# Two buffers for the pieces of an expert table, and routing and first fetches put elsewhere, in an attention and expert kernel on one core

## The reference

```python
x = layernorm(x + attention(x, wq, wk, wv, wo))     # x is (8, 512, 512), f32
                                                    # 16 query heads, 4 key heads, head size 128, causal
x = layernorm(x + ffn(x))

def ffn(x):                                         # xt: 4096 tokens x 512
    logits = clip(xt @ gate_w.T, -50, 50)           # 8 experts
    top_w, top_idx = top_k(logits, 2); rw = softmax(top_w)
    deltas = softmax(expert_atom_weights) @ atoms   # 8 x 4096
    weighted = deltas * sigmoid(importance)
    # each expert is a sparse 512 x 512 matrix: entry s stands at
    # row mask_idx[s] // 512, column mask_idx[s] % 512
    contrib[t] = sum over the 2 experts of rw * (sparse matrix of the expert @ xt[t])
    return xt @ W.T + contrib
```

## Time and profile before

| | before |
|---|---|
| median of 3 runs | 2000.81 us (1997.71 to 2002.41) |
| profiled execution, its own time | 1998.23 us |
| its span, first to last instruction | 1996.4 us |
| mean granted TensorE clock, as a share of full speed | 0.958 |
| busy, of the span | PE 93%, DVE 62%, POOL 46%, ACT 39% |

### The profile page before, as it was taken

The page is one execution under the profiler, slowest core; times in us unless marked ns, Lnnn a source line. Parts: engine busy times, 40 slices in busy tenths (PEclk is TensorE's granted clock), DMA queues, the critical chain, the costliest instruction groups (busy, mean ns, idle before and its releaser), DMA issues.

```text
span 1996.4 us, 34047 instructions
## 1 busy us (share of the span) xinstructions
PE 1855.9 (93%) x9525; PEld 1569.1 (79%) x9525; DVE 1228.6 (62%) x3786; ACT 778.1 (39%) x1985; POOL 925.7 (46%) x1282
## 2 busy tenths in 40 slices
PE   7899999999999999999998999999899988899990
PEld 7788888888888888888887778877788866677770
DVE  4445557776677677667756776677767764543435
ACT  1244444443434444344433333433434432233442
POOL 6366434334443444343435554554432335677763
PEclk6899999999999999999999999999999989899995
DMA  8453363334333433343355554655443285345766
GB/s 287 164 175 121 117 243 117 117 106 149 106 111 101 149 111 122 116 139 106 117 175 154 169 169 148 197 165 163 153 159 139 75 317 195 127 146 201 262 228 269
DMA packets 151974, 318.77 MB, mean 160 GB/s; under 512 B 18904, under 2 KB 62184, under 8 KB 140840
## 3 DMA queue, kind: packets, MB, share of 16 engines
q1 hardware_dynamic: 132320, 273.06, 40.0%
q0 software_dynamic: 19472, 43.49, 7.0%
HBM read 226.38 MB, written 90.12 MB: 159 GB/s over the span
## 4 chain that ended last, share of the span: by engine, by line
PE 64%; POOL 9%; DVE 7%; issue 6%; DMA 6%; ACT 2%; SPq 1%; POOLq 1%; DVEq 0%; ACTq 0%
PE psum L1245 18%; PE psum L1247 17%; PE psum L1246 17%; PE psum L1272 5%; DMA route_rows<-attn_residual 2%; POOL piece_lo L1165 2%; ACT probs L1496 2%; DMA split_expert_weights<-piece_lo 2%; PE psum L1882 2%; PE psum L1883 2%; PE psum L1884 2%; POOL piece_hi L873 1%; POOL token_rows L270 1%; DMA token_rows<-x,ids_now 1%; POOL expert_slots L470 1%
## 5 line engine op out<-in xcount | busy, mean ns | idle before, releaser
L1135 POOL TENSOR_SCALAR probs<-probs,row_inv 128x128 f32<-128x128 f32 (+3 forms) x512 | 306.5, 630 | 422.7 <-DVE row_inv L1598 420.0
L1496 ACT ACTIVATE probs<-probs,neg_max 128x512 f32<-128x512 f32 (+3 forms) x512 | 282.5, 554 | 366.5 <-DVE neg_max L1590 364.4
L1245 PE MATMUL psum<-xT_hi,w_hi 128*128 128x512 f32 x640 | 253.1, 395 | 7.1 <-PEq L622 3.7
L1247 PE MATMUL psum<-xT_hi,w_lo 128*128 128x512 f32 x640 | 250.9, 392 | 0.0
L1246 PE MATMUL psum<-xT_lo,w_hi 128*128 128x512 f32 x640 | 250.4, 391 | 0.0
L1590 DVE CUSTOM_DVE_ANT_0 probs<-psum,causal 128x512 f32<-128x512 f32 (+3 forms) x512 | 223.1, 487 | 32.7 <-PE psum L1247 12.3
L1245 PE MATMUL psum<-wo_hi,oT_hi 128*128 128x512 f32 x512 | 208.3, 407 | 27.0 <-DVE y_acc L1625 26.5
L1601 DVE TENSOR_TENSOR pT_lo<-psum,pT_hi 128x512 fp32r<-128x512 f32 (+1 forms) x384 | 206.5, 593 | 22.6 <-ACT pT_hi L1506 22.3
L1506 ACT CAST pT_hi<-psum 128x512 fp32r<-128x512 f32 (+1 forms) x384 | 172.2, 526 | 90.4 <-PE psum L1272 90.4
L1247 PE MATMUL psum<-wo_hi,oT_lo 128*128 128x512 f32 x512 | 203.9, 398 | 0.0
L1246 PE MATMUL psum<-wo_lo,oT_hi 128*128 128x512 f32 x512 | 203.7, 398 | 0.0
(11 more groups left out here) (200 smaller groups left out, 4054.6 us busy)
## 6 DMA issues: line engine op xcount, KB each, us to landing
w_hi<-split_qk_weights SPq DMA_DIRECT2D x140, 256.0 KB, 2.8
w_lo<-split_qk_weights SPq DMA_DIRECT2D x140, 256.0 KB, 3.2
wo_hi<-split_out_weights SPq DMA_DIRECT2D x28, 1024.0 KB, 4.9
wo_lo<-split_out_weights SPq DMA_DIRECT2D x28, 1024.0 KB, 7.1
expert_weights_hi_lo<-split_expert_weights SPq DMA_DIRECT2D x8, 2048.0 KB, 9.7
x_in<-in_L_attn_x_dram SPq DMA_DIRECT2D x8, 1024.0 KB
expert_weights<-fill_sb SPq DMA_DIRECT2D x4, 2048.0 KB, 8.7
attn_residual<-y_acc SPq DMA_DIRECT2D x8, 1024.0 KB
```

The source lines that it names most:

```text
L1135: last = pool.tensor_scalar(p, p, row_inv[:, buf, i:i + 1], 1.0, ALU.mult, ALU.mult)
L1245: pe.matmul(dst, hi_s, hi_m, start=start, stop=False)
L1247: return pe.matmul(dst, lo_s, hi_m, start=False, stop=stop)
L1496: last = act.activation(probs[:, buf, a:a + w], probs[:, buf, a:a + w], ACT.Exp, bias=neg_max[:, buf, i:i + 1], scale=-1.0, accum_out=row_ ...
```

## The change

1. `piece_hi` and `piece_lo` get two buffers (`piece_raw` moves to other memory to make room), and each store counts on its own semaphore, so that POOL waits for the store of two pieces ago. SP issues the stores of both pieces after its three weight slots, where the first stood between them.
2. On POOL, `normalize(n + 4, 0)` stands ahead of `split_v` and `low_v`, in every iteration that has both.
3. On DVE in the last batch, the three parts of the tile table stand at the ends of the iterations g = 0, 1, 2; before, in the middle of g = 1, 2, 3.
4. In the very last iteration POOL issues the four first token fetches near its top rather than at its end; ACT and DVE make `pT(n + 3)` earlier, ahead of parts of the routing; and the hi and lo parts of the first token tile are made at the iteration's end rather than in the stage of the experts. The buffers of that tile lie in the memory of `causal` and of `v_hi`.
5. In the stage of the experts, one DVE copy of a 128x2 slot (destination and share together, `slot_now`, eight buffers) takes the place of POOL's copy of the destination (L268) and DVE's copy of the share. The last four token tiles are routed in six turns each instead of five: PE's ranks at step 5 instead of 4, DVE's ranks and places at 6 instead of 5, POOL's `route_place` at 7 instead of 6. PE's wait for the last `y_acc` is at the third tile instead of the second.
6. In the tail, the shift of a pair is computed after the variance of the next one.

Left out of the diff: the declarations of the buffers, semaphores and their memory, the same change of wait at two more places, and the new names in `send`, `rows_out` and the matmuls.

```diff
 JT = SEGMENTS * SEG_TILES
-AHEAD, TOKEN_BUFS = 2, 3
+AHEAD, TOKEN_BUFS, SLOT_BUFS = 2, 3, 8
 BANK_RANK, BANK_TURN, BANK_ROWS = 0, 1, 4
...
+def high_tokens(act, E, psum, j):
+
+    act.wait_ge(E.s_turn, j + 1)
+    act.copy(E.xT_hi[j % TOKEN_BUFS][:], psum[:, BANK_TURN + j % 2, :]).then_inc(E.s_hi, 1)
+
+
+def low_tokens(dve, E, psum, j):
+
+    number = dve.value_load(E.tile_number_i[0:1, j:j + 1], min_val=0, max_val=SEG_COLS - 1)
+    dve.wait_ge(E.s_hi, j + 1)
+    dve.tensor_copy(E.slot_now[:, j % SLOT_BUFS], slot_column(E, j, number).rearrange("p a n -> p (a n)")
+                    ).then_inc(E.s_slot_now, 1)
+    dve.tensor_tensor(E.xT_lo[j % TOKEN_BUFS][:], psum[:, BANK_TURN + j % 2, :], E.xT_hi[j % TOKEN_BUFS][:].bitcast(F32),
+                      ALU.subtract).then_inc(E.s_lo, 1)
+
+
 def slot_column(E, j, number):
...
-    k, buf, segment = j % GROUP, j // GROUP % 2, j // SEG_TILES
+    k, segment = j % GROUP, j // SEG_TILES
     if j >= 2 * GROUP:
...
     pool.tensor_copy(E.ids_now[:, k:k + 1], E.token_ids[:, segment, bass.ds(number, 1)]).then_inc(E.s_ids_now, 1)
-    pool.tensor_copy(E.dest_now[:, buf, k:k + 1], slot_column(E, j, number)[:, :, 0]).then_inc(E.s_ids_now, 1)
-    pool.wait_ge(E.s_ids_now, 2 * j + 2)
+    pool.wait_ge(E.s_ids_now, j + 1)
     pool.indirect_dma_start(out=E.token_rows[:, k], out_offset=None,
...
     s_piece_in = [sem(f"piece_{k}_loaded") for k in range(2)]
-    s_piece, s_piece_out = sem("piece_split"), sem("piece_kept")
+    s_piece, s_piece_out = sem("piece_split"), [sem(f"piece_{k}_kept") for k in range(2)]
...
                 dst = kept_pieces[bass.ds((b - SPLIT_BATCHES[0]) * 2 + step // PER_C, 1), step % PER_C, s]
-                sp.dma_start(dst.rearrange("a p e r -> (a p) e r"), half[:].bitcast(F32)).then_inc(s_piece_out, 16)
+                sp.dma_start(dst.rearrange("a p e r -> (a p) e r"), half[:, step % 2].bitcast(F32)
+                             ).then_inc(s_piece_out[step % 2], 16)
...
                 slot(j, it + 2, second)
-                if job == "split" and j == 0:
-                    keep_piece(b, 2 * g)
             if job == "split":
-                keep_piece(b, 2 * g + 1)
+                for half in range(2):
+                    keep_piece(b, 2 * g + half)
             if job == "last":
                 if g == 0:
-                    sp.wait_ge(s_piece_out, 32 * PIECES)
+                    for kept in s_piece_out:
+                        sp.wait_ge(kept, 16 * PIECES)
                     sp.wait_ge(s_v, NB * TT)
...
         def split_piece(b, g, step):
-            number = piece_number(b, step)
-            raw = F.piece_raw[:, step % 2].rearrange("p (r e) -> p e r", e=NE)
-            wait_apart(pool, s_piece_in[step % 2], 16 * ((b - SPLIT_BATCHES[0]) * HKV + g + 1), s_passed)
-            wait_apart(pool, s_piece_out, 32 * number, s_passed)
-            pool_round(pool, F.piece_hi[:], raw).then_inc(s_piece, 1)
+            number, k = piece_number(b, step), step % 2
+            raw = F.piece_raw[:, k].rearrange("p (r e) -> p e r", e=NE)
+            wait_apart(pool, s_piece_in[k], 16 * ((b - SPLIT_BATCHES[0]) * HKV + g + 1), s_passed)
+            wait_apart(pool, s_piece_out[k], 32 * ((b - SPLIT_BATCHES[0]) * HKV + g), s_passed)
+            pool_round(pool, F.piece_hi[:, k], raw).then_inc(s_piece, 1)
             wait_apart(pool, s_piece, 2 * number + 1, s_passed)
-            pool.tensor_tensor(F.piece_lo[:], raw, F.piece_hi[:].bitcast(F32), ALU.subtract).then_inc(s_piece, 1)
+            pool.tensor_tensor(F.piece_lo[:, k], raw, F.piece_hi[:, k].bitcast(F32), ALU.subtract).then_inc(s_piece, 1)
...
             normalize(n + 1, 1)
+            if kind == "end":
+                pool.wait_ge(E.s_ids, 1)
+                pool.wait_ge(E.s_tables, 1)
+                pool.wait_ge(R.s_x1_out, 16 * (SEG_T + 1))
+                for j in range(GROUP):
+                    fetch(pool, R, E, j)
             if kind == "first" and route:
...
                 slot(j, it + 2)
+            if kind != "end":
+                normalize(n + 4, 0)
             if kind in ("first", "group"):
...
                 low_v(g + 1, it + 2)
-            if kind != "end":
-                normalize(n + 4, 0)
             if not route and kind == "batch":
...
             if job == "last" and g == 0:
+                for kept in s_piece_out:
+                    pool.wait_ge(kept, 16 * PIECES)
                 pool.iota(table.tile_at_i[:], pattern=[[1, SEG_TILES]], base=0, channel_multiplier=0).then_inc(E.s_tile_at, 1)
-            if kind == "end":
-
-                pool.wait_ge(E.s_ids, 1)
-                pool.wait_ge(E.s_tables, 1)
-                pool.wait_ge(R.s_x1_out, 16 * (SEG_T + 1))
-                for j in range(GROUP):
-                    fetch(pool, R, E, j)
             if route:
...
                 qT(n + 5, 1, bank_of_query(1, kind))
+            if kind == "end":
+                pT(n + 3, 1)
             if route:
                 route_exp(act, R, it - TT)
-            pT(n + 3, 1)
+            if kind != "end":
+                pT(n + 3, 1)
             oT(n, 1, kind)
...
                 exps(n + 4, 0)
+            else:
+                high_tokens(act, E, psum, 0)
...
             inverse(n + 2, 0)
-            if job == "last":
-                if g == 1:
-                    table_sums_low(dve, E, table)
-                if g == 2:
-                    table_behind(dve, E, table)
             if early:
...
             inverse(n + 3, 1)
-            if kind == "end":
-                table_numbers(dve, E, table)
             if route:
...
             oT(n, 0, 0, kind)
+            if kind == "end":
+                pT(n + 2, 0)
             if route:
...
             if kind == "end":
-                pT(n + 2, 0)
                 add_rows(it - 1, 3, "spare")
             oT(n, 0, 1, kind)
+            if kind == "end":
+                pT(n + 3, 1)
             if route:
...
                 qT(n + 5, 1, bank_of_query(1, kind))
-            pT(n + 3, 1)
-            if kind != "end":
+                pT(n + 3, 1)
                 maxima(n + 4, 0)
...
                 inverse(n + 4, 0)
+            else:
+                low_tokens(dve, E, psum, 0)
             if job == "last" and g == 1:
...
                 add_rows(it, 3, kind)
+            if job == "last" and g < HKV - 1:
+                (table_sums_low, table_behind, table_numbers)[g](dve, E, table)
...
     y_pairs = y_dram[0:2 * CAP, :].rearrange("(c u p t) d -> c u p t d", c=2, p=P, t=2)
-    B, FIRST_ROUTED, ROUTE_STEPS, FIRST_PAIR = SEGMENTS - 1, 4, 5, 11 * GROUP
-    COUNTED = FIRST_ROUTED + ROUTE_STEPS * TT + 3
+    B, FIRST_ROUTED, ROUTE_STEPS, FIRST_PAIR = SEGMENTS - 1, 4, 6, 11 * GROUP
+    COUNTED = FIRST_ROUTED + ROUTE_STEPS * (TT - 1) + 7
     s_used_pool = sem("c_rows_used_by_pool")
...
             step = i - FIRST_ROUTED - ROUTE_STEPS * (tt - LAST)
-            if 0 <= step <= 6:
+            if 0 <= step <= 7:
                 yield tt, step
...
             for tt, step in routed(j):
-                if step == 6:
+                if step == 7:
                     route_place(pool, R, tt)
...
                     pe.wait_ge(E.s_d_in[e], 16)
-            if j == 1:
+            if j == 2:
...
             for tt, step in routed(j):
-                if step == 4:
+                if step == 5:
                     route_ranks(pe, R, tt, B, upper, ones, BANK_RANK)
...
     def scalar(act):
-        def high(j):
-            act.wait_ge(E.s_turn, j + 1)
-            act.copy(E.xT_hi[:, j % TOKEN_BUFS].rearrange("p c n -> p (c n)"), psum[:, BANK_TURN + j % 2, :]).then_inc(E.s_hi, 1)
-
         def rows_out(j):
...
                 act.wait_ge(E.s_y_out[k], 16 * (j // GROUP))
-            act.wait_ge(E.s_share_now, j + 1)
-            act.activation(E.y_rows[:, k], psum[:, BANK_ROWS + k, :], ACT.Copy, scale=E.share_now[:, k:k + 1]).then_inc(E.s_y_sb, 1)
+            act.wait_ge(E.s_slot_now, j + 1)
+            act.activation(E.y_rows[:, k], psum[:, BANK_ROWS + k, :], ACT.Copy, scale=E.slot_now[:, j % SLOT_BUFS, 1:2].bitcast(F32)).then_inc(E.s_y_sb, 1)
...
-        for j in range(AHEAD):
-            low(j)
+        for j in range(1, AHEAD):
+            low_tokens(dve, E, psum, j)
         for j in range(JT):
             if j + AHEAD < JT:
-                low(j + AHEAD)
+                low_tokens(dve, E, psum, j + AHEAD)
             for tt, step in routed(j):
...
                     route_shares(dve, R, tt)
+                if step == 6:
                     route_ranked(dve, R, tt, B, BANK_RANK)
...
             variance(u)
-            shift_of(u)
+            if v:
+                shift_of(u - 1)
+        shift_of(PAIRS + PAIRS_LEFT - 1)
```

(21 more changed lines are left out.)

30 lines of the change are left out of this document (11 added, 19 removed).

## The result

The changed kernel takes 2009.04 us (median of 7 runs, 2007.54 to 2011.42), the kernel before 2000.07 in the same comparison (7 runs, 1997.71 to 2003.02). The ratio is 1.0045, with a 95% interval from 1.0033 to 1.0057: slower by 9 us. The profiled execution took 2008.11, with a span of 2006.3.

The account below looks back on a forecast made before the run. TensorE, busy 1855.9 of 1996.4 us, was taken as the bound, with its waits and lower clock to change. Terms 12.8 + 21.0 - 12 - 3.5 - 5 - 3 + 1 = +11.3 on 1998.23 gave 2009, range 1972 to 2020.

Parts of the forecast that it names:

- Pieces: Split batches 5 and 6: two buffers end the late store, but the second piece holds up DVE; 54.8 instead of 42.0, +12.8 us.
- case A: Rival as summed: DVE is held up by both pieces and by `v_lo`; 2009 us, 2001 to 2020, split batch 218; chance 0.42.
- stall of 4.0 per iteration: Split batches: PE idles 4.0 us in each of four iterations behind held-up L530 and `qT_lo`, plus 1.8 for the clock.
- Order of v: Iteration ends: `v_lo` behind normalize holds up DVE's L563; 1.4 us per iteration, +21.0 outside the split batches, bounds 0 to 22.5.
- Six turns and the copy: Experts' stage: -12 us for four routed tiles (-5 to -15), and -3.5 in turns that carry pairs (0 to -5).
- 0.15 a turn: Experts' stage, turns with pairs: POOL sets the pace in part of them; 23 turns by 0.15, -3.5 us.
- Tail: Shift one pair later removes the wait for `c_rstd` in 7 of 8 pairs; -5 us, between -2 and -7.
- which stays: Tail: POOL's addition holds up other operations, two `c_shift` taking 1.29 us, and this was to remain after the change.
- Turn into the experts and tables: Last batch: earlier token fetches -3 us (-2 to -8); table pieces moved to iteration ends +1 (-2 to +2).
- B: Rival: hold-ups exist, but L530 runs before `piece_lo` and costs nothing; 2000 us, or 1986 with half the v term; chance 0.28.
- C: Rival: idle PE comes from the late store, and the second piece finds DVE's gaps; 1963 us, 1934 to 1979; chance 0.20.
- D: Rival: POOL's waiting and placing per tile keep it behind despite six turns; -5 for -12, 7 us higher; chance another 0.06.

Follow-up runs that it names:

- experiment 1: Kernel before with only the two piece buffers, their waits and the stores behind the weight slots: 2008.08 us, ratio 1.0041.
- experiment 4: Changed kernel with v split ahead of normalize again and POOL's second piece waiting for DVE's conversion and chosen experts: 1946.81 us, ratio 0.9742 against the kernel before.
- experiment 5: Changed kernel with v split ahead of normalize again and, in split batches, DVE's routing and ACT's exponential later: 1934.43 us, ratio 0.968 against the kernel before.
- experiment 9: Kernel before, one piece buffer, with only the routing moved later on DVE and ACT in the split batches: 2003.26 us, ratio 1.0029.
- experiment 3: Changed kernel with the split of v ahead of normalize(n+4,0) again: 1983.64 us, ratio 0.9919 against the kernel before.
- experiment 2: Kernel before with only normalize(n+4,0) moved ahead of the split of v: 2020.34 us, ratio 1.0105.
- experiment 6: Changed kernel with the last four token tiles routed in five turns each again: 2016.01 us, ratio 1.0088 against the kernel before.
- experiment 10: Changed kernel with v split ahead of normalize again and the four first token fetches back at the last iteration's end: 1987.44 us, ratio 0.9945 against the kernel before.
- experiment 8: Changed kernel with the tile table's three parts in the middle of the last batch's iterations again: 2021.3 us, ratio 1.012 against the kernel before.

## Why the prediction was right

2009.04 was measured where 2009 was forecast, and that agreement is luck. The forecast added 11.3 us to the profiled execution's 1998.23; measured are 9.0 between the medians, from 2000.07. And terms that were off by 1 to 4 us cancel within the sum. What the experiments bear out is the account.

- **Pieces.** +12.8 forecast, +11.9 in the two windows, a split batch at 218.2 and 217.8 where case A had 218. The stall of 4.0 per iteration measured 3.8, L530 held up for 2.74 as in case A, and experiments 1, 4, 5 and 9 show the mechanism from both sides. Within a split batch I had 4.2 us for the order of v and 4 x 5.8 = 23.2 for the stall with its lower clock; set against the changed kernel, experiments 1 and 3 give 1.8 to 4.1 for the one and 23.1 to 25.3 for the other. The sign that the busy time rises at a lower clock held: 198.98 at 0.96 against 190.83 at 1.00 in the earlier trace rows. One reading behind the step was wrong: the 0.69 of `qT_lo` in the earlier trace rows does not show that what reads PSUM is not held up, since POOL stood idle beside it. The `pT_lo` of experiment 5 show it.
- **Order of v.** 1.4 forecast for an iteration, 1.33 measured (15.9 / 12). The step named the wrong victim: not the conversion (L563) but the rank product ahead of it was held up, by 1.1 us; the 0.2 of the first rank product was forecast. I had taken the times of the earlier trace rows as fixed, while `v_lo` came at the very moment of the product. In the last batch the term is larger than its 4.2: 7 us in experiment 2, of which 1.6 may not be its doing, and 6.1 between the changed kernel and experiment 3, part of it in the turn into the experts.
- **Six turns and the copy.** -12 and -3.5 forecast; -6.2 and -3.5 by the means under experiment 6, -8.3 and -3.1 by single executions, with the second holding more than the copy. The sum of the stage is -11.4, not -15.5: the first is a term that I sized too large, and its 2.1 for each of the last three tiles came from no row. The 23-tile window hid this: its -11.6 is partly given back behind it, where experiment 6 is 3.5 us faster than the changed kernel. I had also taken the stage to end at 1955, while the last product ends at 1946.2. The window held 8.8 us of the tail, and PE's idle time in the 55 tiles is 7.0 us, not 15.8. The 0.15 a turn that I took for POOL's pace had thus less to work on than I thought, and no run separates it.
- **Tail.** -5 forecast, -8.4 measured, outside my bounds of -2 to -7. The failing step is "which stays": the hold-up of `c_shift` by POOL's addition does not stay, since in its new place it runs during the gap ahead of that addition. A pair costs 2.92 and not 3.5 us. It is the same hold-up as in the rest of the kernel, and I did not carry it through here.
- **Turn into the experts and tables.** -3 and +1 forecast; the fetches' place measures -2.2 to -3.3 (experiment 10). The tables' +1 could not be measured by itself (experiment 8).
- **The rivals.** B and C both hung on L530. It was held up in all eight iterations, so they are out. The prediction's D, that six turns would give 5 us and not 12, was at least as near as A: 6.2, or 8.3 at the most.

With the routing moved out of the pieces' way and v split first, the rest of the change is worth 64 us (1934.43).

What the trace shows of L542, L544, L546 and L577 is what the Trainium skill ("SBUF — State Buffer", section "Who interferes with whom") states: copies, casts and tensor_scalar in two-port modes, and operations of two SBUF inputs beside a GpSimd operation that reads SBUF, are blocked for the whole of a GpSimd operation that issued first. Held up here are a tensor_scalar (L542), a cast (L546) and two operations of two SBUF inputs (L544, L577), each to the end of a GpSimd operation that had begun before it (L546 at 1137.23, behind `piece_lo` at 1137.10). By the same section of the Trainium skill a DVE operation with at most one SBUF input, outside the two-port modes, does not contend with GpSimd. The `pT_lo` beside the pieces in experiment 5 agree (0.67 to 0.68 us), and the maximum L543, which has one SBUF input, was not held up either (0.17 us beside `piece_hi`).

## What to carry to other kernels

A wait that keeps two engines apart can be what protects them from each other: before it is removed, lay the freed work on the other engine's timeline and look at which small operations it will lie on, and at what stands behind these in order. When an engine's busy time rises with the same number of instructions, compare the durations of the small operations by line, and compare their ends with those of the neighbour's large operations. If the transfer can't move, the small operations can: the same early pieces cost 23 to 25 us a batch with the routing beside them, and nothing with it moved behind the second one.

## What the hardware showed that I had not expected

A 128x2 conversion that takes 0.17 us stood for 2.74 us, and the price for PE was larger than that: 3.8 us of idle time and the lower clock for what followed, 0.96 over the batch. That both go away together was not expected either: in experiment 4 PE still waits 4.1 us for `y_acc` and 3.5 for `pT_lo` in the two batches, in pieces of at most 1.2 us, and the granted clock stays at 1.00.
